# Storing v's rows ahead of a head's loads, and spreading twelve weight pieces over six attention heads

## The chip, the cores and the metric

The kernel runs on one core of a Trainium2 chip. The metric is the time of one execution on the device in microseconds (us). TensorE (PE in the rows) multiplies, VectorE (DVE) and ScalarE (ACT) take the products out of PSUM, GpSimd (POOL) adds in SBUF, and SyncE (SP) issues nearly all DMAs from one queue in program order.

## The reference

One transformer block with conditioning, all in float32, for 2 sequences of 2048 rows of 512 values, 16 heads of 32:

```
ada = silu(c) @ Wada + bada            # shifts, scales and gates
h   = ln(x) * (1 + scale_msa) + shift_msa
q, k, v = h @ Wq + bq, h @ Wk + bk, h @ Wv + bv
A   = softmax(q k^T / sqrt(32))        # per sequence and head
x   = x + gate_msa * (A v @ Wo + bo)
h2  = ln(x) * (1 + scale_mlp) + shift_mlp
out = x + gate_mlp * (gelu(h2 @ W1 + b1) @ W2 + b2)
```

## The kernel before

**Three stages.** The first makes q, k and v in 8 chunks of 512 rows (`chunk`; 12 products `m` each: 4 blocks of q, 4 of k, 4 tiles of v). Every operand is split in a rounded part (`hi`) and a remainder (`lo`), and three matmuls make one product. ACT writes the `hi` part of a q or k block and DVE the `lo` part into one of two slots of `qk_st` (slot m % 2), SP stores both; a v tile goes through one of two slots of `v_st`. So a block waits on ACT until the store of the block two before it has landed (`qk_out`), and a v tile waits on DVE for the store of the tile two before (`v_out`). Beside the last two chunks, `first_max` makes the row maxima of head 0's scores.

**Heads.** The second stage runs 32 heads (`G`; "head" is also the name of a function on each engine), each in 16 steps `t` (128 keys against 2048 queries, four groups `r` of 512 in the four row strips of the array). In a step PE makes four score tiles from four matmuls each (lines 1325, 1327, 1329, 1334), four tiles of the next head's first scores (line 1313, two early in the step and two late), and for the step before the product with v (line 1347); after six of the steps (2, 5, 8, 11, 14, 15) it also makes column sums (line 1338) for that step's tile. ACT takes four exponentials a step (line 835), then the sums if any (line 813). DVE takes four maxima a step (line 1042, "a quad"). GpSimd adds the other ten exponential tiles in place, two instructions a tile (line 686). PE's products of the head stage rotate through 7 PSUM banks by a table (`bank_table`, `USES`) that is computed when the program is written: each use names the bank and the use before it that must be over. `EXTRA_AT` lists steps of head 0 in which a second quad is made, so that the maxima run ahead of the scores.

**Loads of a head.** `load_hi(g)` loads q's and k's rounded part (256 KB and 1 MB), `load_lo(g)` the remainders, `load_v(g)` v. `put_max(g)` sends the maxima to their rows. PE waits for `hi_in` before the first maximum tile of a head and for `lo_in` before its first score. SP works through one list, in which a wait holds back everything behind it.

**Weight pieces.** Wo and W1 (`late`, 12 pieces of 128x512) are needed only in the third stage (projection and MLP). Each is loaded into one of two slots of `tmp3`; ACT rounds it (`split_late_hi`, line 795), then DVE subtracts the rounded part from the piece (`split_late_lo`, line 1074, both inputs in SBUF), and the slot is free. These stand in an engine's program behind the work of a step (`between`): in head 0, steps 2 to 13, one in each. The third stage's first projection waits for all of them.

The third stage is not touched by the change.

Of the kernel before, what the change touches and what calls it, by code (L numbers as in the profile page):

```python
# [31 lines left out]
KC = D // P  # L32
FB = FF // P
CH = 512
TT = CH // P
# [14 lines left out]
HALVES = 2  # L50
FILLS = NQ * NT
LEAD = 3
EXTRA_AT = (2, 6, 10)
BANKS, O_BANK = 7, 7
START = 1

# [8 lines left out]
def bank_table():  # L65

    step, group = 11.7, 3.7  # L70
    until = {"S": (8, 10, 12, 14), "M": (11, 13, 6, 8), "D": 16}
    free = [0] * BANKS
    last = [None] * BANKS
    count = {"S": 0, "M": FILLS, "D": 0}

    def use(kind, at, banks):
        bank = min(banks, key=lambda b: free[b])
        free[bank] = at
        before = last[bank]
        count[kind] += 1  # L80
        last[bank] = (kind, count[kind])
        return bank, before, count[kind]

    now = 0
    heads = []
    for g in range(G):
        steps = []
        for t in range(NT):
            tail = g == G - 1
            banks = range(BANKS)  # L90
            uses = {"extra": [], "max": [None] * NQ, "scores": [None] * NQ, "sums": []}
            if g == 0 and t in EXTRA_AT:
                uses["extra"] = [use("M", now + 6 + 3 * n, banks) for n in range(NQ)]
                now += 8
            for pair, others in ((0, 1), (2, 3)), ((2, 3), (0, 1)):
                for r in pair:
                    uses["scores"][r] = use("S", now + until["S"][r], range(3 + r, 4 + r) if tail else banks)
                if g < G - 2 or g == G - 2 and t < NT - LEAD:
                    for r in others:
                        uses["max"][r] = use("M", now + until["M"][r], banks)  # L100
            tiles = [(t - 1) % NT] if (g or t) and (t - 1) % NT in PE_TILES else []
            groups = [PE_TILES.index(tile) for tile in tiles] + ([ND - 1] if g and t == 1 else [])
            for n, d in enumerate(groups):
                uses["sums"].append((d, *use("D", now + until["D"] + 2 * n, range(2, 3) if tail else banks)))
            now += step + group * len(groups)
            steps.append(uses)
        heads.append(steps)
    end = [(d, *use("D", now, range(2, 3))) for d in (PE_TILES.index(NT - 1), ND - 1)]
    return heads, end
# [6 lines left out]
def block_kernel(nc, x, cT, wq, wk, wv, wo, w1, w2, wada, bqT, bkT, b1T, badaT, bada, bv, bo, b2, out):  # L116
# [7 lines left out]
    with ExitStack() as ctx:  # L124
# [206 lines left out]
        def rows_of(w, c0):  # L331
# [14 lines left out]
        late = [(wo[k * P:(k + 1) * P, :], [wo_r[:, s, k, :] for s in range(2)]) for k in range(KC)]  # L346
        late += [(w1[k * P:(k + 1) * P, at:at + D], [w1_r[:, s, k, at:at + D] for s in range(2)])
                 for k in range(KC) for at in range(0, FF, D)]
        LATE_STEP = 2
        N_CONST = 5  # L350


# [21 lines left out]
        def _(sp):  # L374
# [141 lines left out]
            def store_rec(g):  # L516

                sp.wait_ge(rec_ok, g + 1)
                sp.dma_start(rec_dram[g:g + 1, :].rearrange("o (p x) -> (o p) x", x=NT), rec_c[:]).then_inc(rec_out, 16)

            def head(g):

                sp.wait_ge(b_mm, g * FILLS)
                if g + 2 < G:
                    load_hi(g + 2, (g + 2) % HI_BUF)
                load_sums(g - 1)
                sp.wait_ge(pv_mm, START + g * NT)
                load_lo(g + 1, (g + 1) % TWO)
                load_v(g + 1, (g + 1) % TWO)
                store_rec(g - 1)  # L530
                put_max(g + 1, (g + 1) % TWO)
                store_head(g - 1, (g - 1) % TWO)


            store_qk(NCHUNK - 2, *ORDER[NCHUNK - 2], range(2))
# [6 lines left out]
            store_v(NCHUNK - 2, *ORDER[NCHUNK - 2])  # L542
            sp.wait_ge(qkv_mm, (NCHUNK - 1) * MM_CHUNK)
            load_k(k_hi[0], qk_hi, 0, hi_in[0])
            load_k(k_lo[0], qk_lo, 0, lo_in[0])
            store_qk(NCHUNK - 1, *ORDER[NCHUNK - 1])
            store_v(NCHUNK - 1, *ORDER[NCHUNK - 1], range(1))
            sp.wait_ge(a_max, FILLS)
            load_q(q_hi[0], qk_hi, 0, hi_in[0])
            put_max(0, 0)  # L550
            load_hi(1, 1)
            store_v(NCHUNK - 1, *ORDER[NCHUNK - 1], range(1, TT))
            for k, (rows, _) in enumerate(late):
                if k == 0:
                    sp.wait_ge(ada_mm, ADA)
                if k >= 2:
                    sp.wait_ge(late_hi, k - 1)
                    sp.wait_ge(late_lo, k - 1)
                sp.dma_start(tmp3[:, k % 2, :], rows).then_inc(late_in[k % 2], 16)
                if k == 1:  # L560
                    sp.wait_ge(qkv_mm, NCHUNK * MM_CHUNK)
                    stored(NCHUNK)
                    load_v(1, 1)
                    load_hi(2, 2)
                    load_lo(1, 1)
            put_max(1, 1)
            for g in range(1, G - 2):
                head(g)

# [152 lines left out]
        def _(act):  # L722
# [116 lines left out]
                    if t in between:  # L839
                        between[t]()  # L840

            probs(0, {LATE_STEP + k: lambda k=k: split_late_hi(k) for k in range(len(late))})
            for i in range(2):
                act.wait_ge(v_out[i], START + 16 * NCHUNK * TT // 2)
            for g in range(1, G - 1):
                probs(g)

            def split_first_oT(half):

# [46 lines left out]
        def _(dve):  # L896
# [177 lines left out]
                nc.vector.tensor_tensor(lo, tmp3[:, k % 2, :], hi.bitcast(F32), ALU.subtract).then_inc(late_lo, 1)  # L1074


            head(0, {LATE_STEP + k: lambda k=k: split_late_lo(k) for k in range(len(late))})
            for g in range(1, G - 1):
                head(g)

            def normalise_first(half):
                dve.wait_ge(oT_in, 16 * half + 16)
# [433 lines left out]
```

## Time and profile before

| | |
|---|---|
| median of 3 runs | 2544.93 us (2541.89 to 2549.74) |
| the profiled execution, its own time | 2552.45 us |
| its span in the trace | 2550.7 us |
| PE busy | 2414.3 us (95%) |
| DVE, POOL, ACT busy | 68%, 59%, 56% |

Read it as one engine, PE, that works nearly all the time, and look for the stretches where it doesn't. In the page's 40 slices (64 us each) PE is at 9 tenths but for the first slice, slices 5 to 8 from the left (from about 255 us to 510 us) and the end of the head stage near 2050 us. The granted clock (PEclk) is below full in the same places.

### The profile page before, as it was taken

To read this page: it belongs to the slowest core of one execution; us is meant where nothing else is said; L and a number is where in the kernel's file an instruction comes from. 1 tells how busy PE (TensorE), PEld (TensorE's weight loads), DVE (VectorE), ACT (ScalarE), POOL (GpSimd) and SP (SyncE) were. 2 spreads that over 40 slices of the span, in tenths; PEclk is the share of its full clock that TensorE was granted. 3 is DMA by queue.
4 is the path that set the end of the run, shared out by engine and by line. 5 is a ranking of instruction groups with operands and counts; after the bars stand their busy time and mean duration, and the time that the engine had idled before them with its cause. 6 is when DMAs were issued, how large, how long until landed. Compare 5 with 4: busy or idle time off the path is not lost.

```text
span 2550.7 us, 49502 instructions
## 1 busy us (share of the span) xinstructions
PE 2414.3 (95%) x19544; PEld 1358.2 (53%) x19544; DVE 1745.4 (68%) x2878; ACT 1423.4 (56%) x2622; POOL 1502.3 (59%) x706
## 2 busy tenths in 40 slices
PE   6999855899999999999999999999999888999998
PEld 4788642344444444444444444444444346888887
DVE  4444544788888888887888888788878326666563
ACT  3233203577777777777777777777777542222221
POOL 0000103488788878887887888788878634232330
PEclk9999986799999999999999999999999888999999
DMA  7655532122222222222222222222222111332200
GB/s 268 208 171 186 137 110 89 45 75 58 67 72 71 58 68 72 66 62 69 75 57 66 75 69 57 67 77 62 61 71 74 49 50 39 93 103 68 66 34 34
DMA packets 204948, 210.33 MB, mean 82 GB/s; under 512 B 112384, under 2 KB 145152, under 8 KB 195328
## 3 DMA queue, kind: packets, MB, share of 16 engines
q1 hardware_dynamic: 202224, 205.56, 26.9%
q8 instruction: 143, 2.34, 0.4%
q10 hardware_dynamic: 2512, 1.86, 0.3%
q14 instruction: 69, 0.57, 0.1%
HBM read 146.30 MB, written 60.82 MB: 81 GB/s over the span
## 4 chain that ended last, share of the span: by engine, by line
PE 83%; DMA 8%; DVE 3%; ACT 3%; issue 2%; SPq 1%; POOL 0%; ACTq 0%; POOLq 0%; DVEq 0%
PE ps L1216 19%; PE ps L1347 19%; PE ps L1313 9%; PE ps L1325 9%; PE ps L1456 7%; PE ps L1338 7%; PE ps L1327 5%; PE ps L1329 4%; DMA partial_sums<-work 4%; PE ps L1334 2%; DMA q_lo<-work 2%; DVE part_max L1042 1%; ACT work L813 1%; PE ps L1225 1%; DMA tmp<-in_wo 1%
## 5 line engine op out<-in xcount | busy, mean ns | idle before, releaser
L686 POOL TENSOR_TENSOR work<-work 128x1024 f32<-128x1024 f32 x576 | 1351.5, 2405 | 413.9 <-PE ps L1338 223.1
L1042 DVE TENSOR_REDUCE part_max<-ps 128x1 f32<-128x512 f32 x1984 | 1233.2, 682 | 287.7 <-PE ps L1313 287.5
L835 ACT ACTIVATE work<-ps 128x512 f32<-128x512 f32 x2048 | 1058.4, 603 | 355.2 <-PE ps L1334 323.3
L1347 PE MATMUL ps<-work 128*32 128x512 f32 x4096 | 557.7, 617 | 0.2 <-ACT work L835 0.2
L1313 PE MATMUL ps<-acts_r 32*128 32x512 f32 x1344 | 419.2, 480 | 24.7 <-DVE part_max L1042 18.7
L1216 PE MATMUL ps<-acts_r,weights_r 128*128 128x512 f32 x1536 | 383.6, 400 | 4.9 <-DVE acts_r L962 3.8
L1216 PEld LDWEIGHTS ps<-acts_r,weights_r 128*128 128x128 f32 x1536 | 293.5, 193 | 70.2 <-issue 6.8
L1325 PE MATMUL ps<-acts_r 32*128 32x512 f32 x1408 | 300.9, 475 | 28.9 <-DVE work L975 20.0
L1325 PEld LDWEIGHTS ps<-acts_r 32*128 32x128 f32 x1408 | 145.8, 187 | 339.4 <-DVE part_max L1042 176.6
L1327 PE MATMUL ps<-acts_r 32*128 32x512 f32 x1408 | 260.9, 401 | 0.0
L1313 PEld LDWEIGHTS ps<-acts_r 32*128 32x128 f32 x1344 | 181.5, 186 | 140.5 <-DVE part_max L1042 111.4
L1338 PE MATMUL ps<-work,ones 128*32 128x512 f32 x1792 | 236.8, 600 | 0.0
L1334 PE MATMUL ps<-acts_r,minus_r 1*128 1x512 f32 x1024 | 232.7, 450 | 0.0
L1334 PE MATMUL ps<-m_odd,minus_r 1*128 1x512 f32 x1024 | 227.8, 441 | 0.0
L884 ACT ACTIVATE work<-ps,b_sb 128x512 f32<-128x512 f32 x64 | 44.0, 689 | 309.0 <-PE ps L1216 309.0
L1313 PE MATMUL ps<-acts_r,w_r 32*128 32x512 f32 x640 | 199.0, 474 | 7.0 <-DVE part_max L1042 4.1
L1216 PE MATMUL ps<-weights_r,acts_r 128*128 128x512 f32 x768 | 188.7, 400 | 12.9 <-DVE acts_r L1092 9.9
L659 POOL TENSOR_TENSOR var_eps<-var_eps,mv 128x4 f32<-128x4 f32 x16 | 3.2, 201 | 320.4 <-DVE mv L940 320.4
L1329 PE MATMUL ps<-w_r,acts_r 32*128 32x512 f32 x1024 | 188.2, 402 | 0.0
L1329 PE MATMUL ps<-acts_r 32*128 32x512 f32 x1024 | 186.0, 396 | 0.0
L701 POOL TENSOR_TENSOR work<-work,gate_b 128x512 f32<-128x512 f32 x60 | 85.6, 1456 | 170.0 <-DMA work<-in_x 149.6
L1456 PE MATMUL ps<-w_r,acts_r 128*128 128x512 f32 x768 | 184.4, 391 | 0.0
(88 smaller groups left out, 2542.9 us busy)
## 6 DMA issues: line engine op xcount, KB each, us to landing
acts_r<-k_hi SPq DMA_DIRECT2D x32, 1024.0 KB
acts_r<-k_lo SPq DMA_DIRECT2D x32, 1024.0 KB
work<-in_x SPq DMA_DIRECT2D x16, 1024.0 KB, 5.4
q_hi<-work SPq DMA_DIRECT2D x32, 256.0 KB, 2.6
q_lo<-work SPq DMA_DIRECT2D x32, 256.0 KB, 3.3
k_hi<-work SPq DMA_DIRECT2D x32, 256.0 KB, 2.6
k_lo<-work SPq DMA_DIRECT2D x32, 256.0 KB, 3.2
v_rows<-work SPq DMA_DIRECT2D x32, 256.0 KB, 2.0
```

The lines of the kernel that those rows point to most:

```text
L686: nc.gpsimd.tensor_tensor(psum_acc[:, at], first, prob[:, t % RING, at], ALU.add).then_inc(add_ok, 1)
L835: nc.scalar.activation(prob[:, t % RING, j * CH:(j + 1) * CH], ps[:, bank, :], ACT.Exp, scale=SCALE).then_inc(exp_ok, 1)
L1042: nc.vector.tensor_reduce(part_max[:, r * TT + q // NQ, q % NQ:q % NQ + 1], ps[:, bank, :], AX.X, ALU.max).then_inc(a_max, 1)
L1216: mm = nc.tensor.matmul(o, lhs(s, kk), rhs(r, kk), start=(kk == 0 and s == r), stop=(kk == KC - 1 and s == 1))
L1313: nc.tensor.matmul(ps[:, use[0], :], q_hi[u][at, q // NQ * P:(q // NQ + 1) * P], k_hi[u][at, q % NQ * CH:(q % NQ + 1) * CH], start=True, s ...
L1325: nc.tensor.matmul(o, k_hi[u][at, keys], q_hi[u][at, :], start=True, stop=False)
L1327: nc.tensor.matmul(o, k_lo[w][at, keys], q_hi[u][at, :], start=False, stop=False)
L1329: nc.tensor.matmul(o, k_hi[u][at, keys], q_lo[w][at, :], start=False, stop=False)
L1334: nc.tensor.matmul(o, minus_r[row, :], m_row[w][row, :], start=False, stop=True).then_inc(b_mm, 1)
L1338: mm = nc.tensor.matmul(ps[j * DH:(j + 1) * DH, bank, :], ones[:, 0:DH], src(j), start=True, stop=True)
L1347: mm = nc.tensor.matmul(ps[j * DH:(j + 1) * DH, O_BANK, :], v_sb[g % TWO][:, t, :], prob[:, t % RING, j * CH:(j + 1) * CH], start=(t == 0) ...
L1456: mm = nc.tensor.matmul(ps[:, 4 + t, :], g_r[:, f % 4, s, t * P:(t + 1) * P], w2_r[:, r, f, :], start=(f == 0 and s == r), stop=(f == FB - ...
```

## The change

It does five things. The v stores of the last chunk are issued around `put_max(0)` and ahead of `load_hi(1)`. The last chunk's q stores are issued between `load_k(k_hi[0])` and `load_k(k_lo[0])`. Head 1's v and remainders are loaded ahead of head 2's rounded parts. The twelve weight pieces go two to a head, heads 0 to 5, behind steps 4 and 11 (`LATE_STEPS`), loaded at the end of the SP work of the head before. And head 0 makes no maximum tiles in step 0, and a second quad in steps 3, 6, 9 and 12 in place of 2, 6 and 10.

```diff
-EXTRA_AT = (2, 6, 10)
+EXTRA_AT = (3, 6, 9, 12)
...
-                if g < G - 2 or g == G - 2 and t < NT - LEAD:
+                if (g or t) and g < G - 2 or g == G - 2 and t < NT - LEAD:
...
-        LATE_STEP = 2
+        LATE_STEPS = (4, 11)
+        LATE_HEADS = len(late) // len(LATE_STEPS)
...
+            def load_late(g):
+
+                for k in range(g * len(LATE_STEPS), (g + 1) * len(LATE_STEPS)):
+                    if k >= 2:
+                        sp.wait_ge(late_hi, k - 1)
+                        sp.wait_ge(late_lo, k - 1)
+                    sp.dma_start(tmp3[:, k % 2, :], late[k][0]).then_inc(late_in[k % 2], 16)
+
             def head(g):
...
                 store_head(g - 1, (g - 1) % TWO)
+                if g + 1 < LATE_HEADS:
+                    load_late(g + 1)
...
             load_k(k_hi[0], qk_hi, 0, hi_in[0])
+            store_qk(NCHUNK - 1, *ORDER[NCHUNK - 1], range(KC))
             load_k(k_lo[0], qk_lo, 0, lo_in[0])
-            store_qk(NCHUNK - 1, *ORDER[NCHUNK - 1])
+            store_qk(NCHUNK - 1, *ORDER[NCHUNK - 1], range(KC, 2 * KC))
             store_v(NCHUNK - 1, *ORDER[NCHUNK - 1], range(1))
             sp.wait_ge(a_max, FILLS)
             load_q(q_hi[0], qk_hi, 0, hi_in[0])
+            store_v(NCHUNK - 1, *ORDER[NCHUNK - 1], range(1, 3))
             put_max(0, 0)
+            store_v(NCHUNK - 1, *ORDER[NCHUNK - 1], range(3, TT))
             load_hi(1, 1)
-            store_v(NCHUNK - 1, *ORDER[NCHUNK - 1], range(1, TT))
-            for k, (rows, _) in enumerate(late):
...
-                if k == 1:
-                    sp.wait_ge(qkv_mm, NCHUNK * MM_CHUNK)
-                    stored(NCHUNK)
-                    load_v(1, 1)
-                    load_hi(2, 2)
-                    load_lo(1, 1)
+            sp.wait_ge(ada_mm, ADA)
+            load_late(0)
+            sp.wait_ge(qkv_mm, NCHUNK * MM_CHUNK)
+            load_v(1, 1)
+            load_lo(1, 1)
+            load_hi(2, 2)
+            stored(NCHUNK)
             put_max(1, 1)
+            load_late(1)
...
-            probs(0, {LATE_STEP + k: lambda k=k: split_late_hi(k) for k in range(len(late))})
+            def late_pieces(g):
+                first = g * len(LATE_STEPS)
+                return {t: lambda k=first + i: split_late_hi(k) for i, t in enumerate(LATE_STEPS) if g < LATE_HEADS}
+
+            probs(0, late_pieces(0))
...
-            head(0, {LATE_STEP + k: lambda k=k: split_late_lo(k) for k in range(len(late))})
-            for g in range(1, G - 1):
-                head(g)
+            for g in range(G - 1):
+                first = g * len(LATE_STEPS)
+                head(g, {t: lambda k=first + i: split_late_lo(k) for i, t in enumerate(LATE_STEPS) if g < LATE_HEADS})
```

On SP, at the end of the last chunk, the list stood like this before; `v_rows` is where v is stored, `q_hi` and `k_hi` are where a head's parts are loaded from, `max_T` the maxima, and `in_wo` a weight piece:

```order
L430 DMA v_rows<-work 128x512
L482 DMA acts_r<-q_hi 128x1x512
L500 DMA acts_r<-max_T 4x4x32 x4
L482 DMA acts_r<-q_hi 128x1x512
L478 DMA acts_r<-k_hi 128x1x2048
L430 DMA v_rows<-work 128x512 x3
L559 DMA tmp<-in_wo 128x512 x2
```

and now:

```order
L431 DMA v_rows<-work 128x512
L483 DMA acts_r<-q_hi 128x1x512
L431 DMA v_rows<-work 128x512 x2
L501 DMA acts_r<-max_T 4x4x32 x4
L431 DMA v_rows<-work 128x512
L483 DMA acts_r<-q_hi 128x1x512
L479 DMA acts_r<-k_hi 128x1x2048
L528 DMA tmp<-in_wo 128x512 x2
```

The last three v tiles are stored ahead of head 1's q and k, the weight pieces still behind them.

On DVE, from the end of head 0 to the middle of head 1, the list stood like this before (`part_max` is a maximum, x4 a quad, `weights_r` the subtraction of a weight piece, `sums_c` and `den_c` the denominators of step 8):

```order
L994 STREAM_TRANSPOSE max_T<-row_max 128x32
L1074 TENSOR_TENSOR weights_r<-tmp,weights_r 128x512
L1042 TENSOR_REDUCE part_max<-ps 128x1 x4
L1074 TENSOR_TENSOR weights_r<-tmp,weights_r 128x512
L1042 TENSOR_REDUCE part_max<-ps 128x1 x44
L1052 TENSOR_REDUCE den_c<-sums_c 128x16
```

and now:

```order
L1006 STREAM_TRANSPOSE max_T<-row_max 128x32
L1054 TENSOR_REDUCE part_max<-ps 128x1 x32
L1086 TENSOR_TENSOR weights_r<-tmp,weights_r 128x512
L1054 TENSOR_REDUCE part_max<-ps 128x1 x16
L1064 TENSOR_REDUCE den_c<-sums_c 128x16
L1066 RECIPROCAL rec_c<-den_c 128x16
L1054 TENSOR_REDUCE part_max<-ps 128x1 x12
L1086 TENSOR_TENSOR weights_r<-tmp,weights_r 128x512
```

The two last subtractions of head 0 are gone, and head 1 has one between the quads of steps 4 and 5 and one between those of steps 11 and 12. Heads 2 to 5 read as head 1.

## Rows read from the trace of the kernel before

**Rows 1.** The page: busy time by engine, share of the span, instructions.

```profile
PE 2414.3 (95%) x19544; PEld 1358.2 (53%) x19544; DVE 1745.4 (68%) x2878; ACT 1423.4 (56%) x2622; POOL 1502.3 (59%) x706
```

**Rows 2.** Busy time by stretches: from, to, length, engines, PEclk, DMA share, GB/s.

```profile
330.00:340.00 10.00, 0.00 (x0) 0.00 (x0) 0.00 (x0) 0.67 (x1) 0.00 (x0) 0.50 0.23 93
...
560.00:680.00 120.00, 119.25 (x1212) 53.66 (x1208) 97.64 (x165) 90.33 (x173) 103.88 (x45) 1.00 0.25 70
```

**Rows 3.** Timeline, last chunk: start, length, engine, line, [idle before <-releaser].

```profile
310.53 0.58 SPq L478 DMA_DIRECT2D acts_r<-k_hi  x1
...
339.33 0.69 ACT L763 ACTIVATE work<-ps,bq_sb 128x512 fp32r<-128x512 f32 x1 [22.00 <-DMA q_lo<-work]
...
341.45 0.79 PE L1256 MATMUL ps<-acts_r 96*128 96x512 f32 x1 [18.31 <-DVE part_max L980]
...
345.74 0.43 SPq L425 DMA_DIRECT2D q_lo<-work  x1
...
356.56 0.69 ACT L763 ACTIVATE work<-ps,bq_sb 128x512 fp32r<-128x512 f32 x1 [3.05 <-PE ps L1216]
```

**Rows 4.** Timeline, from the last chunk to head 0.

```profile
374.52 0.55 SPq L478 DMA_DIRECT2D acts_r<-k_hi  x1
375.11 18.55 SPq L430 DMA_DIRECT2D v_rows<-work  x3
392.61 0.69 DVE L975 TENSOR_TENSOR work<-ps,work 128x512 f32<-128x512 f32 x1 [21.07 <-DMA v_rows<-work]
393.40 0.79 PE L1325 MATMUL ps<-acts_r 32*128 32x512 f32 x2 [19.99 <-DVE work L975]
```

**Rows 5.** Timeline, first step of heads 1 and 4: the output of the head before.

```profile
497.07 0.60 ACT L801 ACTIVATE work<-ps 128x512 f32<-128x512 f32 x1 [0.19 <-PE ps L1338]
...
648.38 0.60 ACT L801 ACTIVATE work<-ps 128x512 f32<-128x512 f32 x1 [0.28 <-PE ps L1338]
```

**Rows 6.** Timeline, head 0: the wait for a late piece, and pieces beside GpSimd.

```profile
429.57 0.63 ACT L795 ACTIVATE weights_r<-tmp 128x512 fp32r<-128x512 f32 x1 [10.30 <-DMA tmp<-in_wo]
...
453.58 0.69 DVE L1074 TENSOR_TENSOR weights_r<-tmp,weights_r 128x512 fp32r<-128x512 f32 x1 [0.46 <-ACT weights_r L795]
...
475.41 7.44 POOL L686 TENSOR_TENSOR work<-work 128x1024 f32<-128x1024 f32 x3 [4.05 <-ACT work L835]
...
478.23 2.42 DVE L1074 TENSOR_TENSOR weights_r<-tmp,weights_r 128x512 fp32r<-128x512 f32 x1 [2.01 <-ACT weights_r L795]
...
481.30 0.79 PE L1313 MATMUL ps<-acts_r,w_r 32*128 32x512 f32 x1 [3.59 <-DVE part_max L1042]
...
487.61 1.94 PE L1347 MATMUL ps<-work 128*32 128x512 f32 x8
...
491.50 1.06 PE L1347 MATMUL ps<-work 128*32 128x512 f32 x8
```

**Rows 7.** Timeline, head 3, steps 3 to 5, and its GpSimd work.

```profile
607.30 37.45 POOL L686 TENSOR_TENSOR work<-work 128x1024 f32<-128x1024 f32 x16 [1.15 <-ACT work L835]
...
608.92 2.48 DVE L1042 TENSOR_REDUCE part_max<-ps 128x1 f32<-128x512 f32 x4 [1.10 <-PE ps L1313]
...
609.75 2.07 ACT L835 ACTIVATE work<-ps 128x512 f32<-128x512 f32 x4 [0.64 <-POOL work L686]
...
610.11 1.06 PE L1347 MATMUL ps<-work 128*32 128x512 f32 x8
...
611.66 2.48 DVE L1042 TENSOR_REDUCE part_max<-ps 128x1 f32<-128x512 f32 x4 [0.25 <-PE ps L1313]
...
612.83 1.06 PE L1347 MATMUL ps<-work 128*32 128x512 f32 x8
```

**Rows 8.** Timeline, head 2, around the denominators of step 8.

```profile
571.29 1.06 PE L1347 MATMUL ps<-work 128*32 128x512 f32 x8
...
572.51 0.35 DVE L1052 TENSOR_REDUCE den_c<-sums_c 128x16 f32<-128x112 f32 x1
...
574.18 1.07 PE L1347 MATMUL ps<-work 128*32 128x512 f32 x8
```

More of the change, by code:

```diff
@@ L549, in _ @@
             load_q(q_hi[0], qk_hi, 0, hi_in[0])
+            store_v(NCHUNK - 1, *ORDER[NCHUNK - 1], range(1, 3))
             put_max(0, 0)
+            store_v(NCHUNK - 1, *ORDER[NCHUNK - 1], range(3, TT))
             load_hi(1, 1)
-            store_v(NCHUNK - 1, *ORDER[NCHUNK - 1], range(1, TT))
-            for k, (rows, _) in enumerate(late):
[L554 to L559, printed above, removed]
-                if k == 1:
-                    sp.wait_ge(qkv_mm, NCHUNK * MM_CHUNK)
-                    stored(NCHUNK)
-                    load_v(1, 1)
-                    load_hi(2, 2)
-                    load_lo(1, 1)
+            sp.wait_ge(ada_mm, ADA)
[5 more added lines that the diff above has]
+            stored(NCHUNK)
             put_max(1, 1)
+            load_late(1)
             for g in range(1, G - 2):
@@ L845, in _ @@
             for g in range(1, G - 1):
-                probs(g)
+                probs(g, late_pieces(g))
             def split_first_oT(half):
```

## The prediction

> **What bounds the kernel now.** I read the page first: PE is busy 2414.3 us, 95% of the span [rows 1], so only stretches in which PE waits or runs slowly can give time. The stretches show which those are: from 560 us on, in the middle of the heads, PE works 119.25 of 120 us at full clock, with POOL busy 103.88 and DVE 97.64 [rows 2]. That part has nothing to give, and anything added to it that reaches PE is a loss. Then I read the timeline where PE is idle.
>
> Three waits stand out, all behind 1 MB loads. First, in the last chunk, ACT waits 22.00 us for a store of q and PE 18.31 us [rows 3]: SP issued head 0's k_hi and k_lo at 310.5 us, and the q stores land behind both. Second, PE waits 19.99 us for the last v tile, because the v stores, issued from 375.1 us, stand behind head 1's q_hi and k_hi (374.5); the v tile is taken at 392.6 [rows 4]. Third, in head 0 ACT waits 10.30 us for a weight piece behind two more such loads [rows 6]. After each wait the granted clock is at its lower level, 0.50, which is 1.2 GHz [rows 2].
>
> A head in the steady part takes (648.38 - 497.07) / 3 = 50.4 us, while head 0 takes 497.07 - 393.40 = 103.7 us, both up to the same instruction in the next head [rows 4, 5]. So head 0 holds 53 us of loss, and 12 weight pieces.
>
> My unit for loads: from the issue of k_hi(1) at 374.52 to the v tile at 392.61 are 18.1 us for 1.25 MB, or 14 us for 1 MB with its start [rows 4].
>
> **Term 1, q stores between k_hi(0) and k_lo(0): -6 us.** The first q store now waits for 1 MB and not 2. ACT resumed at 339.3; it will at about 326, 13.3 us earlier. The k_lo load is then issued behind the fourth q store, at 345.7 - 13.3 = 332.4, later by the issue, about 333, and lands with the store behind it at about 348.6. The block that needs that store is the seventh; ACT took it at 356.56 [rows 3], 343.3 when moved by 13.3. So it comes 5.3 us late, and PE waits about 4.7 for it (in the wait that we have, 22.00 us less the usual 3.05 make ACT 18.95 us late and PE waits 18.31, 0.6 less). The second wait costs a second stretch at the lower clock, some 5 us with half the speed, 2.5 us. 13.3 - 4.7 - 2.5 = 6. Range 3 to 10.
>
> **Term 2, v stores first: -4 us.** This step does what it says and gains little. The second v store is now issued at about 369.5 and only q_hi(0), 256 KB, is ahead of it; the last v tile is taken at about 374.5, and head 0 begins there, not at 393.4. But step 1 needs head 1's q_hi and k_hi, whose issue moves from 374.5 to about 376. They were the load that all had to wait for, and they still take 14 to 17 us: step 1 begins at about 393. What is saved is one step 0, 4 us at the lower clock. The wait for the v store becomes a wait for `hi_in`.
>
> **Term 3, head 0 without ten pieces and the 10.30 us wait: -29 us.** From step 1 at 393 to the output in head 1: a steady head is 50.4 us, less step 0 and plus the part of the next head's step 0 up to its output, nearly equal. Four extra quads of 2.48 us against 1.10 us of DVE idle in a step with sums [rows 7]: 5.5. Two pieces at 5.0 (below): 10. Lower clock at the start and behind the extra quads: 4.7, my choice between nothing and the 10 us or so of four stretches like the one priced below. Sum 70.6, so it ends at 463.6, against 497.07: 33.5 earlier, 4 of them term 2. Head 2's loads, 2.5 MB behind head 1's, land at about 431, before step 13 needs them at about 447. Range of terms 2 and 3: 26 to 41.
>
> **Term 4, ten pieces in heads 1 to 5: +50 us.** This decides. In step 4 of a steady head [rows 7], ACT ends its exponentials at 609.75 + 2.07 = 611.8. The rounding, 0.63 us, ends at 612.45, and DVE, free since 608.92 + 2.48 = 611.4, has waited. Its next quad was due at 611.66. The subtraction then meets GpSimd. Row 478.23 shows what happens: GpSimd ran three additions of 2.34 us from 475.41, with ends at 477.75 and 480.1; the subtraction started at 478.23 and took 2.42 us, to 480.65, 0.55 behind the end of an addition, where one with GpSimd idle took 0.69 [rows 6]. The eleven others of head 0 read the same way. In a steady head GpSimd adds without a gap from 607.30 for 37.45 us, sixteen additions, over steps 4 and 11 both [rows 7]. The one that runs at 612.5 ends at 614.3; the subtraction ends at 614.9, and the quad is 3.2 us late.
>
> What PE has in hand against that is almost nothing. The denominators put 0.6 us on DVE, which has 0.25 us idle a step, and PE's step grew from 612.83 - 610.11 = 2.72 to 574.18 - 571.29 = 2.89 [rows 7, 8]. The reason is in the bank table: in step 5 the last maximum tile takes the bank of the first one of the same step. So PE waits about 3.1 us. By row 481.30, where the subtraction was held too, it was 3.59 us. Then the clock: behind that wait a step took 491.50 - 487.61 = 3.89 us, mostly at the lower level, against 2.72 [rows 6], and such a stretch lasts one or two steps, 1.2 to 2.5 us. Sum 5.0 a piece. At step 11 GpSimd is on its queue of additions as well, with a delay by the same count of about 3.0 us. Ten pieces: 50 us. Bounds: no meeting with GpSimd leaves the quad 1.5 us late, 15 us for ten; a full addition of delay each time and two slow steps is 57.
>
> The Trainium skill (SBUF — State Buffer, "SBUF: two separate sides") has the rule: GpSimd and a VectorE instruction with two SBUF inputs share a pair of ports, whichever starts first holds it for its whole instruction, and the other is blocked. The trace agrees, 2.42 against 0.69 us. By the rule each moved piece is exposed, since GpSimd is busy 103.88 of 120 us in a steady stretch [rows 2]; without it the ten would cost about 15 us and the change would be a gain of 24.
>
> **Parts at nothing.** ACT's 0.63 us of rounding lies in its idle 0.6 us before the next exponentials (without it, +0.6 us a piece, hidden behind DVE's delay). The loads of pieces, 512 KB a head, are issued near step 12, when the head's own 2.5 MB (34 us by my unit) are in; were they late, ACT would wait as at 429.57. SP's new waits in `load_late` are for steps 4 and 11, over by `put_max` at step 12, so nothing queues behind them. The bank table repeats as before from head 3 on.
>
> **Sum.** -6 - 4 - 29 + 50 = +11 us on the profiled execution's 2552.45. The median of the runs shown is 7.5 us below that execution; I carry the difference over: 2544.9 + 11 = 2556.
>
> **The rivals.** *A, forecast: pieces cost about 5 us each in the steady heads, and outweigh head 0's gain.* Chance 0.5; -5 to +20 us.
> *B, the clock holds.* If the waits of 3.1 us don't bring the lower clock, or only for a moment, term 4 is 31 and the sum -8: 2537. For it: the steady heads run at 1.00 throughout [rows 2], so the engine is well used before each wait. Against it: the wait of 3.59 us in head 0 was followed by matmuls at half speed, 1.94 us for the eight of line 1347 that take 1.06 otherwise [rows 6]. Chance 0.15.
> *C, the pieces hide, and the change is faster.* The place is the subtraction behind step 4: if the phase of GpSimd's additions is such that one ends as DVE asks, the quad is 1.5 to 2 us late and term 4 is about 20 to 25. The sum is then -16: 2529. It decides below a price of 3.9 us a piece (39 us gained over ten). For it: PE's waits shift PE against GpSimd and may open gaps. Against it: additions have no gap from 607.3, so the phase at step 4 is the same in each head. Chance 0.15.
> *D, head 0 gives less.* If the second wait in the last chunk is as long as the first, or the lower clock holds through head 0's extra quads as it did before, terms 1 to 3 give 25 and the sum is +25: 2570. For it: head 0 has 53 us of loss before, and what of it belongs to its pieces, to its three extra quads and to the clock I can't separate. Chance 0.2.
>
> **How the numbers follow.** The predicted time is A's, 2556. The range, 2529 to 2573, takes in B, most of C and D. About 0.3%, 7.6 us, is what a measurement of this kernel can tell from no change. Faster by more needs -8 or less: most of C and half of B, 0.2. Within: the lower part of A and the rest of B, 0.22. Slower: 0.58.
>
> **What would show it.** Right: PE's wait before the first step of head 0 gone, one of about 15 us before line 1313's first tile of head 1; ACT's wait for a q store near 10 us and a second of about 5; head 0 to its output in about 70 us from step 1; subtractions of 2 to 3 us in heads 1 to 5, each followed by a PE wait near 3 us on a maximum; heads 1 to 5 about 60 us long, later ones 50.4; PEclk below full between 500 and 750 us. Wrong: subtractions of 0.69 us there, or heads 1 to 5 under 57 us long.

## The result

| | median us | lowest to highest | ratio to before, 95% interval |
|---|---|---|---|
| before, 4 runs beside the others | 2543.41 | 2540.25 to 2549.74 | |
| the changed kernel, 4 runs | 2572.94 | 2566.53 to 2576.44 | 1.0109 [1.0083, 1.0135] |

The change makes the kernel about 28 us slower by the ratio (the two medians are 29.5 us apart). The two profiled executions are nearer to each other: 2569.98 us after (span 2568.2) against 2552.45 before, +17.5. The one of before lies about 9 us above the median of this table, the one of after 3 below; what follows divides up the 17.5.

From the page of the changed kernel, busy time by engine, which answers to [rows 1]:

```profile
PE 2416.8 (94%) x19544; PEld 1356.7 (53%) x19544; DVE 1760.0 (69%) x2878; ACT 1424.0 (55%) x2622; POOL 1506.1 (59%) x706
```

PE does the same work and has 15 us more idle time in a longer span. DVE is 15 us busier with the same 2878 instructions: some of them take longer. To find where, I took the marker of [rows 5], the output of a head in the first step of the next, after head 0 and after head 5 (timeline of the changed kernel):

```profile
470.48 0.60 ACT L809 ACTIVATE work<-ps 128x512 f32<-128x512 f32 x1 [0.21 <-PE ps L1350]
...
771.61 0.60 ACT L809 ACTIVATE work<-ps 128x512 f32<-128x512 f32 x1 [0.26 <-PE ps L1350]
```

The first stands at 497.07 us before [rows 5]: 26.6 us are gained up to there. Heads 1 to 5 then take 62.4, 58.2, 62.0, 60.2 and 58.2 us, 301.1 together, against 250.9 before: +50.2. Heads 6 to 31 come out 4.7 us shorter, 2.4 of it in the last one (single heads vary from 49.7 to 51.0 us in either trace, the last two apart), what is behind them 1.4. The sum is -26.6 + 50.2 - 4.7 - 1.4 = +17.5.

The timeline of the last chunk, which answers to [rows 3]:

```profile
309.88 0.59 SPq L479 DMA_DIRECT2D acts_r<-k_hi  x1
...
328.88 0.69 ACT L771 ACTIVATE work<-ps,bq_sb 128x512 fp32r<-128x512 f32 x1 [12.19 <-DMA q_lo<-work]
...
331.00 0.80 PE L1268 MATMUL ps<-acts_r 96*128 96x512 f32 x1 [8.50 <-DVE part_max L992]
...
335.77 0.56 SPq L479 DMA_DIRECT2D acts_r<-k_lo  x1
...
356.29 0.69 ACT L771 ACTIVATE work<-ps,bq_sb 128x512 fp32r<-128x512 f32 x1 [13.59 <-DMA k_lo<-work]
...
358.42 0.79 PE L1268 MATMUL ps<-acts_r 96*128 96x512 f32 x1 [9.95 <-DVE part_max L992]
```

One wait of PE became two, 8.50 and 9.95 us, 18.45 together against 18.31. ACT takes its seventh block at 356.29, where it took it at 356.56.

From there to head 0, which answers to [rows 4]:

```profile
376.76 0.69 DVE L987 TENSOR_TENSOR work<-ps,work 128x512 f32<-128x512 f32 x1 [3.57 <-DMA v_rows<-work]
377.56 0.81 PE L1337 MATMUL ps<-acts_r 32*128 32x512 f32 x4 [2.49 <-DVE work L987]
378.49 0.54 SPq L479 DMA_DIRECT2D acts_r<-k_hi  x1
...
398.52 0.80 PE L1337 MATMUL ps<-acts_r 32*128 32x512 f32 x2 [18.88 <-DMA acts_r<-k_hi]
```

Head 0 begins at 377.56 and not at 393.40, does step 0, and waits 18.88 us for head 1's k_hi. Step 1 begins at 398.52. Before it began at 397.49, 4.1 us behind 393.40.

The twelve subtractions together (group of the line: shortest, median, longest in ns, first and last start in us), and the first of head 1 with what follows it:

```profile
L1086 DVE TENSOR_TENSOR weights_r<-tmp,weights_r x12: 1117/2448/4897, 416.4 to 752.5; 128x512 fp32r<-128x512 f32 x12
```

```profile
481.57 7.45 POOL L694 TENSOR_TENSOR work<-work 128x1024 f32<-128x1024 f32 x3
...
484.27 2.53 DVE L1086 TENSOR_TENSOR weights_r<-tmp,weights_r 128x512 fp32r<-128x512 f32 x1 [0.95 <-ACT weights_r L803]
...
487.46 0.79 PE L1325 MATMUL ps<-acts_r,w_r 32*128 32x512 f32 x1 [3.02 <-DVE part_max L1054]
...
488.18 1.94 PE L1359 MATMUL ps<-work 128*32 128x512 f32 x8
```

This is the forecast's chain, link by link: DVE waits for ACT's rounding, the subtraction is held beside GpSimd's additions, PE waits 3.02 us for the maximum behind it, and the next matmuls run at the lower level, 1.94 us against 1.06. The piece of step 11 in the same head shows something that the forecast did not have:

```profile
505.05 9.34 POOL L694 TENSOR_TENSOR work<-work 128x1024 f32<-128x1024 f32 x4
...
510.50 4.44 DVE L1086 TENSOR_TENSOR weights_r<-tmp,weights_r 128x512 fp32r<-128x512 f32 x1 [0.89 <-ACT weights_r L803]
...
515.60 0.79 PE L1325 MATMUL ps<-acts_r,w_r 32*128 32x512 f32 x1 [4.88 <-DVE part_max L1054]
...
516.46 1.08 ACT L843 ACTIVATE work<-ps 128x512 f32<-128x512 f32 x2 [4.78 <-PE ps L1346]
...
517.62 2.35 POOL L694 TENSOR_TENSOR work<-work 128x1024 f32<-128x1024 f32 x1 [3.22 <-ACT work L843]
```

GpSimd's four additions end at 507.4, 509.7, 512.1 and 514.4 us (9.34 / 4 each). The subtraction was there from 510.50, yet it did not end 0.55 us behind the addition that was running (512.1) but 0.55 behind the next (514.4): 514.94. Two of the ten pieces in heads 1 to 5 went so, with 4.44 and 4.90 us; the others took 1.7 to 2.5. Both times the subtraction ended only when GpSimd had no addition left: here its next one came at 517.62, after 3.22 us without work, because ACT's exponentials had waited 4.78 us for PE, and PE for the quad behind the subtraction.

Over heads 1 to 5 as a stretch (columns as in [rows 2]), and the ten microseconds around the wait of 4.88 us:

```profile
480.00:740.00 260.00, 228.77 (x2151) 99.45 (x2151) 197.81 (x298) 165.85 (x316) 185.84 (x79) 0.91 0.23 67
```

```profile
510.00:520.00 10.00, 5.12 (x36) 1.28 (x28) 7.27 (x7) 2.64 (x5) 6.75 (x3) 0.68 0.00 0
```

PE works 88% of it and not 99%, and its granted clock is 0.91 on average where the steady part had 1.00.

### The profile page after: what moved, and what is told of

The parts are those of the page before. It is cut to its first block, busy times and chain, and to the rows that moved or that the text cites. A ratio compares the mean times of both kernels' runs of the same rounds, so it can differ in the third digit from the quotient of the medians.

```text
span 2568.2 us, 49501 instructions
## 1 busy us (share of the span) xinstructions
PE 2416.8 (94%) x19544; PEld 1356.7 (53%) x19544; DVE 1760.0 (69%) x2878; ACT 1424.0 (55%) x2622; POOL 1506.1 (59%) x706
## 4 chain that ended last, share of the span: by engine, by line
PE 81%; DMA 7%; DVE 4%; ACT 3%; issue 2%; POOL 1%; SPq 1%; ACTq 0%; POOLq 0%; DVEq 0%
PE ps L1359 18%; PE ps L1228 18%; PE ps L1325 9%; PE ps L1337 9%; PE ps L1350 7%; PE ps L1468 7%; PE ps L1339 5%; PE ps L1341 4%; DMA partial_sums<-work 3%; PE ps L1346 2%; DVE part_max L1054 1%; DMA q_lo<-work 1%; ACT work L843 1%; DVE weights_r L1086 1%; ACT work L821 1%
## 5 line engine op out<-in xcount | busy, mean ns | idle before, releaser
L843 ACT ACTIVATE work<-ps 128x512 f32<-128x512 f32 x2048 | 1059.0, 602 | 395.2 <-PE ps L1346 364.5
L1228 PE MATMUL ps<-weights_r,acts_r 128*128 128x512 f32 x768 | 187.6, 398 | 14.8 <-DVE acts_r L1104 11.8
L821 ACT ACTIVATE work<-ps 128x512 f32<-128x512 f32 x224 | 134.3, 599 | 92.5 <-PE ps L1350 83.9
```

What stands on the lines that cost most here:

```text
L843: nc.scalar.activation(prob[:, t % RING, j * CH:(j + 1) * CH], ps[:, bank, :], ACT.Exp, scale=SCALE).then_inc(exp_ok, 1)
L1228: mm = nc.tensor.matmul(o, lhs(s, kk), rhs(r, kk), start=(kk == 0 and s == r), stop=(kk == KC - 1 and s == 1))
```

## The experiments

### Which half of the change costs, and what a piece's price is made of

**e1: the pieces alone.** The order of SP, the quads and head 0's step 0 of before, the pieces spread as in the change.

```diff
-EXTRA_AT = (3, 6, 9, 12)
+EXTRA_AT = (2, 6, 10)
...
             load_k(k_hi[0], qk_hi, 0, hi_in[0])
-            store_qk(NCHUNK - 1, *ORDER[NCHUNK - 1], range(KC))
             load_k(k_lo[0], qk_lo, 0, lo_in[0])
-            store_qk(NCHUNK - 1, *ORDER[NCHUNK - 1], range(KC, 2 * KC))
+            store_qk(NCHUNK - 1, *ORDER[NCHUNK - 1])
...
             load_hi(1, 1)
+            store_v(NCHUNK - 1, *ORDER[NCHUNK - 1], range(1, TT))
...
```

> The kernel before with only the weight pieces moved: two to a head behind steps 4 and 11 of heads 0 to 5; stores, loads and extra quads as before. Theory (the moved pieces are the loss): heads 1 to 5 take about 60 us each from output to output, 50 us more together, and head 0 gets back 20 to 30 us, so the time is about 2543 + 25 = 2568 us. Rival (the new order of stores and loads, not the pieces, loses): 2543 us or less, heads 1 to 5 near 50 us.

Measured: 2570.77 us, 1.0097 [1.0067, 1.0127]. Its first output is at 464.4 us, 32.7 before that of [rows 5], and heads 1 to 5 take 299.4 us, +48.5. So the pieces alone make the loss, and they also bring all of head 0's gain, 6 us more of it than the whole change.

**e2: the order alone.** The change, with the twelve pieces back in head 0's steps 2 to 13.

```diff
-        LATE_STEPS = (4, 11)
-        LATE_HEADS = len(late) // len(LATE_STEPS)
+        LATE_STEPS = tuple(range(2, 14))
+        LATE_HEADS = 1
...
             load_hi(2, 2)
             stored(NCHUNK)
+            load_late(range(2, len(late)))
...
```

> The changed kernel with all twelve pieces back in head 0, steps 2 to 13; stores, loads and extra quads as changed. Theory (pieces are the loss, the new order gains a little): heads 1 to 5 at 50 us, head 0 longer than in the changed kernel by about 30 us, time about 2540 to 2550 us. Rival (the order loses): over 2560 us.

Measured: 2552.02 us, 1.0021 [1.0008, 1.0034]. The first output is at 499.8 us, 2.8 later than before, and the heads behind it take 50.0. In its last chunk ACT waits 12.2 and 14.2 us, and PE waits 20.3 us for head 1's k_hi. The new order gains nothing; with the pieces in head 0 it is a loss of 0.1 to 0.3%.

**e3: the same place, one SBUF input.** DVE reads only the piece, in a maximum along its rows, in place of the subtraction. The remainders of Wo and W1 are left out.

```diff
-                nc.vector.tensor_tensor(lo, tmp3[:, k % 2, :], hi.bitcast(F32), ALU.subtract).then_inc(late_lo, 1)
+                nc.vector.tensor_reduce(scrap[:, k:k + 1], tmp3[:, k % 2, :], AX.X, ALU.max).then_inc(late_lo, 1)
```

> The changed kernel with the subtraction of a weight piece on VectorE replaced by a maximum over the same 512 elements of the loaded piece: the same place, the same wait for ScalarE, but one input in SBUF in place of two; the remainders of Wo and W1 are left out. Theory (the port pair shared with GpSimd is the larger part): the instruction takes 0.6 to 0.7 us each time, the quad behind it is 1.5 us late, heads 1 to 5 take 53 to 55 us each, time about 2572 - 28 = 2545 us. Rival (the wait for ScalarE in VectorE's program is the cost, the port is not): instruction short, heads still near 60 us, time within 5 us of the changed kernel.

Measured: 2536.51 us, 0.9959 [0.9940, 0.9978]. The group of its line, and the stretch of heads 1 to 5:

```profile
L1087 DVE TENSOR_REDUCE scrap<-tmp x12: 685/686/689, 416.8 to 720.0; 128x1 f32<-128x512 f32 x12
```

```profile
480.00:740.00 260.00, 246.96 (x2444) 108.73 (x2446) 203.57 (x341) 189.14 (x360) 203.86 (x87) 0.98 0.25 70
```

Twelve instructions of 685 to 689 ns beside the same additions of GpSimd: with one SBUF input none is held. Heads 1 to 5 take 268.5 us, 32.7 less than with the subtraction, 3.3 us a piece.

**e4: the subtraction on GpSimd.** It stands there ahead of the additions of two of the steps; DVE has no piece in its program.

```diff
+            def split_late_lo(k):
+                pool.wait_ge(late_hi, k + 1)
+                hi, lo = late[k][1]
+                nc.gpsimd.tensor_tensor(lo, tmp3[:, k % 2, :], hi.bitcast(F32), ALU.subtract).then_inc(late_lo, 1)
+
             for g in range(G - 1):
-                sum_probs(g)
+                first = g * len(LATE_STEPS)
+                sum_probs(g, {t: lambda k=first + i: split_late_lo(k) for i, t in enumerate((6, 12)) if g < LATE_HEADS})
```

> The changed kernel with the subtraction of a weight piece done by GpSimd, ahead of its additions of tiles 6 and 12, and nothing of it on VectorE. Theory: VectorE has neither the wait nor the port conflict, GpSimd takes 1.2 us more twice a head and has 8 us idle in one, so heads 1 to 5 take 50 to 52 us and the time is about 2572 - 45 = 2527 us. Rival (ScalarE's 0.6 us or the loads of pieces are part of the cost): heads 1 to 5 over 55 us. Rival (GpSimd becomes the bound): ScalarE waits for GpSimd's additions in steps 8 to 15, heads 1 to 5 at 53 to 55 us.

Measured: 2513.98 us, 0.9868 [0.9839, 0.9898].

```profile
L699 POOL TENSOR_TENSOR weights_r<-tmp,weights_r x12: 1287/1306/1349, 425.6 to 705.3; 128x512 fp32r<-128x512 f32 x12
```

```profile
480.00:740.00 260.00, 259.21 (x2631) 116.36 (x2635) 211.92 (x356) 201.68 (x387) 233.85 (x105) 1.00 0.26 76
```

PE works 259.21 of 260 us at full clock, and heads 1 to 5 take 248.8 us, no more than heads without a piece. This is the zero against which the others are priced: the subtraction on DVE costs 301.1 - 248.8 = 52.3 us, 5.2 a piece, of which 3.3 is the meeting with GpSimd (e3 against the change) and 2.0 is what DVE's slot costs without it (e3 against e4): a wait for ACT's rounding, and 0.69 us of work.

### Is the rest the wait for ACT, and is the order worth anything without the pieces?

**e5: DVE's part a step later.** ACT rounds behind step 4 as before; DVE subtracts behind step 5.

```diff
-                head(g, {t: lambda k=first + i: split_late_lo(k) for i, t in enumerate(LATE_STEPS) if g < LATE_HEADS})
+                head(g, {t + 1: lambda k=first + i: split_late_lo(k) for i, t in enumerate(LATE_STEPS) if g < LATE_HEADS})
```

> The changed kernel with VectorE's subtraction one step later (steps 5 and 12) while ScalarE's rounding stays at 4 and 11: VectorE no longer waits for ScalarE, but still needs the port pair. Theory (two costs add: about 1.8 us a piece for the wait behind ScalarE, about 3.3 us for the port): the first goes, heads 1 to 5 take 50 + 2 x 3.3 = 56 to 57 us, time about 2572 - 17 = 2555 us. Rival (the place makes the port wait, a wait for ScalarE moves the subtraction onto a fresh addition): heads near 53 us, 2540. Rival (nothing gained, since the port wait ends with an addition whenever it starts): heads 59 to 61 us.

Measured: 2562.95 us, 1.0058 [1.0036, 1.0080]; heads 1 to 5 take 294.8 us, 6.3 less than in the change, where the theory wanted some 17. Its subtractions as a group:

```profile
L1086 DVE TENSOR_TENSOR weights_r<-tmp,weights_r x12: 821/1907/7381, 418.6 to 739.0; 128x512 fp32r<-128x512 f32 x12
```

The wait for ACT is gone. But the ten pieces of heads 1 to 5 now fall into two kinds. The five behind step 5 took 0.82 to 0.88 us: each started about 0.3 us before an addition ended. The five behind step 12 took 7.30 to 7.38 us: each started 0.14 to 0.24 us after an addition had begun, and was held over that one and the two behind it, until GpSimd had none left. One of the long ones with what followed it, then one of the short ones, and the stretches around a short and a long one (timeline of e5, and columns as in [rows 2]):

```profile
502.55 7.35 DVE L1086 TENSOR_TENSOR weights_r<-tmp,weights_r 128x512 fp32r<-128x512 f32 x1
...
510.56 0.79 PE L1325 MATMUL ps<-acts_r 32*128 32x512 f32 x1 [6.47 <-DVE part_max L1054]
...
512.58 2.36 POOL L694 TENSOR_TENSOR work<-work 128x1024 f32<-128x1024 f32 x1 [3.23 <-ACT work L843]
...
540.07 0.88 DVE L1086 TENSOR_TENSOR weights_r<-tmp,weights_r 128x512 fp32r<-128x512 f32 x1
```

```profile
530.00:556.00 26.00, 25.63 (x260) 11.37 (x254) 21.79 (x37) 20.14 (x40) 24.83 (x11) 1.00 0.31 86
556.00:582.00 26.00, 19.51 (x176) 8.45 (x172) 21.24 (x26) 12.81 (x26) 15.16 (x7) 0.80 0.13 39
```

PE waits 0.3 us behind a short one and 6.4 to 6.5 us behind a long one. So e5's loss against e4, 46 us or 9.2 a head, lies nearly all behind step 12, and the same subtraction on DVE behind step 5 costs next to nothing. Neither of the two rivals had that: heads of 58.2 to 60.4 us look like the last one, but the price is not the same whenever the instruction starts. One piece a head behind step 5, over twelve heads, was not run.

**e6: the old order, with GpSimd's subtraction.** The edit of e4 on top of e1.

> The kernel before with the pieces spread and subtracted on GpSimd; stores, loads and extra quads as before. With the fourth run it tells what the new order of stores, loads and quads is worth when the pieces cost nothing. Theory (the new order trades its waits one for one, -4 us by the prediction's terms 1 and 2 and +3 to +6 by the comparison of the first two runs): within 6 us of the fourth run's 2514, ACT's wait for a q store again near 22 us and the v wait near 20, no wait on head 1's k_hi. Rival (the new order is worth its 10 us): 2524 us or more.

Measured: 2510.03 us, 0.9866 [0.9844, 0.9888], beside 0.9868 for e4. ACT waits 23.7 us for the q store and DVE 22.2 us for the v store, much as before the change (22.0 and 21.1).

**e7: e4 with both k loads ahead of the q stores.**

```diff
             load_k(k_hi[0], qk_hi, 0, hi_in[0])
-            store_qk(NCHUNK - 1, *ORDER[NCHUNK - 1], range(KC))
             load_k(k_lo[0], qk_lo, 0, lo_in[0])
-            store_qk(NCHUNK - 1, *ORDER[NCHUNK - 1], range(KC, 2 * KC))
+            store_qk(NCHUNK - 1, *ORDER[NCHUNK - 1])
```

> The fourth run's kernel with one thing undone: both k loads of head 0 go ahead of the last chunk's q stores again. Theory (two waits of 12 to 14 us in place of one of 22: term 1 is nothing or a loss): one ACT wait of 22 to 24 us there, time equal to the fourth run's 2514 or up to 5 us less. Rival (term 1 as predicted): 6 us more, 2520.

Measured: 2508.53 us, 0.9850 [0.9827, 0.9872]. With one wait of ACT of 22.1 us in place of two of 12.7 and 14.7 it is, if anything, 5 us faster than e4; the intervals overlap. Term 1 of the forecast, -6, isn't there.

With e1, e2, e4 and e6 the change is taken apart:

| ratio to before | pieces in head 0, on DVE | spread, on DVE | spread, on GpSimd |
|---|---|---|---|
| old order | 1 | 1.0097 (e1) | 0.9866 (e6) |
| new order | 1.0021 (e2) | 1.0109 (the change) | 0.9868 (e4) |

Each step down is 0.0002 to 0.0021; the effect lies in where the pieces stand and which engine subtracts. Pieces in head 0 with the subtraction on GpSimd were not run, so how much of the gain is the spreading and how much the engine is not split up.

### Why the new order gives nothing: the 1 MB loads

In the wait of the last chunk of before, from 325 us, k's two parts are under way, with the q stores behind them (stretch of before; a k load writes 32 rows of k to four groups of 32 partitions, in one transfer):

```profile
325.00:335.00 10.00, 0.00 (x0) 0.00 (x0) 0.00 (x0) 0.00 (x0) 0.00 (x0) 0.59 0.25 102
```

The DMA share is 0.25, four of 16 engines, at 102 GB/s. The changed kernel has the same 0.25, at 83 GB/s, while it waits for head 1's k_hi:

```profile
386.00:396.00 10.00, 0.00 (x0) 0.00 (x0) 0.00 (x0) 0.00 (x0) 0.00 (x0) 0.50 0.25 83
```

The Trainium skill (DMA: Bandwidth & Descriptors, "Why a DMA increments its semaphore by 16 and not by 1") has a rule for it: a transfer runs on the largest number of engines, up to 16, that divides the slowest dimension of both its sides. For this pattern, whose slowest dimension is the four copies, that is four; the trace agrees, 0.25. So I cut the load in four of 32 rows each.

**e8: e4 with every k load in four transfers.** The counts that PE waits for go up with it.

```diff
-LOADS_HI, LOADS_LO, LOADS_0 = 2, 3, 6
+LOADS_HI, LOADS_LO, LOADS_0 = 5, 6, 6
...
-                rows = src[1][g * DH:(g + 1) * DH, :].rearrange("(o d) q -> o d q", o=1).broadcast_to((NQ, DH, L))
-                sp.dma_start(dst.bitcast(F32), rows).then_inc(done, 16)
+                for r in range(NQ):
+                    sp.dma_start(dst[r * DH:(r + 1) * DH, :].bitcast(F32), src[1][g * DH:(g + 1) * DH, :]).then_inc(done, 16)
```

> The fourth run's kernel with each 1 MB k load issued as four transfers of 32 rows in place of one whose outermost dimension is the fourfold repeat. Theory (one transfer of k uses 4 of the 16 DMA engines, and every wait at the start of the heads is 14 to 20 us long for that): a k load lands in 4 to 6 us, the waits for q stores, k stores and head 1's k_hi fall to under 5 us each, and the time is about 2514 - 35 = 2480 us, if SyncE's 0.55 us for each more issue (24 more a head) stays hidden. Rival (the source's bandwidth bounds the load, not the number of engines): waits within 3 us of the fourth run's, same time. Rival (the loads now take all 16 engines and the partial sums' small transfers wait behind them): heads longer than 50 us.

Measured: 2568.96 us (2547.96 to 2583.91, 12 runs), 1.0081 [1.0055, 1.0106]. The first output came at 431.2 us, 37 earlier than in e4, but the heads behind it take 50.1 to 55.0 us, 52.7 on average and not 50.1 (the last two left out), which takes it all back and more. The wait for head 1's k_hi is 12.0 us, not the under 5 that were expected. The chain that ended last says which transfer is in the way (shares of the span by line):

```profile
PE ps L1227 18%; PE ps L1358 18%; DMA partial_sums<-work 10%; PE ps L1336 9%; PE ps L1324 9%; PE ps L1467 7%; PE ps L1349 6%; PE ps L1338 5%; PE ps L1340 4%; PE ps L1345 2%; ACT work L827 1%; DVE part_max L1060 1%; PE ps L1236 1%; DMA q_lo<-work 1%; DMA work<-in_x 0%
```

The small store of a head's column sums stands in the chain once a head, with 7 to 9.5 us each, 10% in all; in e4 it has 4%. My reading is that the wide loads now keep all 16 engines busy, so that this store finds none free; no run changed that store alone.

**e9: only the first loads in four.** k's rounded part for heads 0 to 2 and its remainder for heads 0 and 1; the single transfer from there on.

```diff
-            def load_k(dst, src, g, done):
+            def load_k(dst, src, g, done, split_heads=3):
+                if g < split_heads:
+                    for r in range(NQ):
+                        sp.dma_start(dst[r * DH:(r + 1) * DH, :].bitcast(F32), src[1][g * DH:(g + 1) * DH, :]).then_inc(done, 16)
+                    return
...
```

> The fourth run's kernel (pieces spread, subtracted on GpSimd, the changed order) with the 1 MB k loads of heads 0, 1 and 2 alone issued as four transfers of 32 rows; from head 3 on single transfers. Theory (the eighth run gained 37 us at the start and lost more in the heads, because its small partial sums waited behind loads on all 16 engines): first output at about 431 us, heads at 49.7 to 50 us, time about 2511 - 37 = 2475 us. Rival (the loss in the heads comes from SyncE's issues or from the first heads' loads): heads over 51 us, time over 2490 us.

Measured: 2481.92 us, 0.9754 [0.9738, 0.9770]. First output at 431.7 us, heads 1 to 5 of 49.8 us. In the last chunk ACT's wait for the q store is gone and that for the k store is 4.4 us, where e4 had 12.7 and 14.7; PE's wait for k_hi is 12.2 us, where e4 had 23.3 (timeline of e9):

```profile
355.37 1.90 SPq L481 DMA_DIRECT2D acts_r<-k_hi  x4
...
367.89 0.79 PE L1341 MATMUL ps<-acts_r 32*128 32x512 f32 x2 [12.21 <-DMA acts_r<-k_hi]
```

**e10: q's first loads in four too.**

```diff
+                if g < split_heads:
+                    for r in range(NQ):
+                        sp.dma_start(dst[r * DH:(r + 1) * DH, :].bitcast(F32), src[0][g * DH:(g + 1) * DH, r * CH:(r + 1) * CH]).then_inc(done, 16)
+                    return
...
```

> The same with the 256 KB q loads of those heads in four transfers too. Theory (q's loads also use 4 of 16 engines and stand ahead of k's): PE's wait for head 1's parts falls from 12 us by some 3 us, time 3 us less than the run with k alone, about 2472 us. Rival (the wait is then SyncE's issue time, 0.35 to 0.5 us a transfer): no less, or more.

Measured: 2475.84 us (2475.06 to 2476.90), 0.9722 [0.9709, 0.9735], the fastest of all. The first loads as a stretch, and the wait for k_hi:

```profile
310.00:316.00 6.00, 6.00 (x28) 4.85 (x27) 5.03 (x8) 1.38 (x2) 0.00 (x0) 1.00 1.00 251
```

```profile
361.79 0.79 PE L1345 MATMUL ps<-acts_r 32*128 32x512 f32 x2 [7.31 <-DMA acts_r<-k_hi]
```

All 16 engines, 251 GB/s, and a wait of 7.31 us where e4 had 23.27 and the change 18.88.

**e11: e9 in the old order.** The edits of e1 and e9 on e4.

> The kernel before with the pieces spread and subtracted on GpSimd and the same split loads of heads 0 to 2, in the old order of stores, loads and quads. It tells what the new order is worth once a load is short. Theory (the order trades waits one for one while each load is 15 to 20 us; with loads of 5 us the old order still has both k loads ahead of the q stores and head 1's parts ahead of the v stores): 5 to 10 us more than the new order, about 2482 us. Rival (the order is worth nothing in either case): within 4 us of the new order's.

Measured: 2486.28 us, 0.9765 [0.9749, 0.9781]. DVE waits 14.8 us for the v store. The new order is 4.4 us faster (e9) in this setting, which the overlapping intervals don't quite settle.

## Why the prediction was right, and where it was not

The direction was right, and so was the mechanism of the loss. The time is in the range by luck: 2572.94 against 2556 (2529 to 2573) is 0.06 us inside the upper end, and two of the four executions lie above it. It was rival D, with a chance of 0.2, that came true, and not forecast A: D had terms 1 to 3 give 25 us and not 39, through a second wait in the last chunk as long as the first; the trace shows that wait, and 26.6 us up to head 0's output. D's +25 stands against +23.6 up to the end of head 5.

**Term 4, ten pieces, +50: right.** Measured +50.2 between the two traces, and 52.3 with e4 as the zero. The chain was as described, and the wait per piece on average too: 3.2 us, forecast 3.1. What I had not foreseen is its spread: five waits of 3.0 us behind step 4 (forecast 3.1), but behind step 11 three of 2.4 and two of 4.88 and 5.29, where the piece was held over two additions. That the five average 3.5, near the 3.0 that I had put there, is luck. The lower bound was too low: "no meeting with GpSimd leaves the quad 1.5 us late, 15 us for ten". Without the meeting e3 still lost 19.7 us, since a late quad of 1.5 us costs clock too (0.98). Rivals B and C fall for the change: the clock did not hold (0.91), and no PE wait was under 2.4 us. But C's mechanism exists: e5's five pieces behind step 5 each met the end of an addition and hid. The argument against C, that the phase is the same in each head, holds in e5 as well; there it is the good phase that repeats.

**Term 3, head 0 without ten pieces, -29: right.** Forecast from step 1 to the output 70.6 us; measured 470.48 - 398.52 = 72.0. That is 31.7 less than the 103.7 of before, of which 4.1 are step 0: 27.6.

**Term 2, v stores first, -4: right in mechanism, nothing gained.** The wait for the v store did become one for `hi_in`. But the unit of 14 to 17 us was too small: k_hi(1) was issued at 378.49 and PE went on at 398.52, 20.0 us later (23.6 in e4). The load no longer had the queue nearly for itself: two weight pieces and v, 768 KB, were issued right behind it, at 379.08 to 380.08 us, and the first ten us of the wait read

```profile
380.00:390.00 10.00, 0.00 (x0) 0.00 (x0) 0.00 (x0) 3.05 (x5) 0.00 (x0) 0.50 0.64 128
```

with more than k_hi's quarter of the engines at work. That they slow k_hi down fits, but no run held them back.

**Term 1, q stores between the two k loads, -6: wrong.** The step that failed is "it comes 5.3 us late, and PE waits about 4.7 for it". ACT resumed at 328.88 (forecast 326) and then waited 13.59 us, PE 9.95. Behind the step is "my unit for loads": 14 us for 1 MB, taken from one wait. Both k loads run on four engines at 83 to 102 GB/s, by my estimate from these rates 10 to 13 us each for the bytes alone; from the issue of one alone to the block that needs a store behind it passed 19.0 us (309.88 to 328.88) and 20.5 (335.77 to 356.29), against 28.8 for both in a row before [rows 3]. So two parted loads take 10.7 us more than the two in a row; that this is a start paid twice is my reading. Terms 1 and 2, forecast at -10, came to +1.0: step 1 at 398.52 where it was 397.49.

The forecast's sum of terms was +11 and the traces say +17.5. The 6.5 between them are 11.0 in terms 1 and 2 and 1.6 in terms 3 and 4, less the 4.7 and 1.4 behind head 5. The median is off by more, 2572.94 - 2556 = 16.9, because I had carried over 7.5 us between the profiled execution and the median of before: behind the change the profiled execution lay 3.0 us below its median, not above.

**Open.** What decides that DVE's instruction is held over one addition or over two or three is not shown. In all eight cases (two in the change, one in e1, five in e5) it was held until GpSimd had no addition left; in the others it was held over one at most, and where another was queued that one then took 2.8 us and not 2.36. Why 1 MB on four engines came at 83 GB/s in one place and 102 in another I did not separate, nor how much of the 18 to 24 us is start or other loads. That the store of sums in e8 is late because no DMA engine is free was argued, not tried.

## What to carry to other kernels

Work that is taken off a starved start has to go to an engine and a place that have time for it in the steady part: here DVE's 0.69 us cost PE 5.2 us each, while the same subtraction, as 1.3 us on GpSimd, cost nothing and turned +1% into -1.3%. And price it place by place, not by the average: a step later, the same DVE instruction cost nearly nothing in one half of the head and 9 us in the other. Look at the DMA share of a stretch in which everything waits for one load: here 0.25 said that the transfer's shape, not its place in the queue, was what to change. And make a load wide only where something waits for it: done in all heads, the heads grew from 50.1 to 52.7 us and the gain was gone.

## What the runs showed of the hardware

- A DVE instruction with two SBUF inputs was held by GpSimd's additions: in the change most often until 0.55 us behind the end of the one that ran, but in two of ten until behind the next (4.44 and 4.90 us), and in five of ten in e5 until behind the third (7.30 to 7.38 us). Each of these longer ones, and one in e1 (4.91), ended 0.55 us behind the last addition before GpSimd ran out of them. An addition that follows such a subtraction directly took 2.8 us in place of 2.36. The Trainium skill (SBUF — State Buffer, "SBUF: two separate sides") gives the port to whichever starts first; the trace agrees that it is held for a whole instruction, but it also shows that one who waits can be passed over by later ones. With one SBUF input nothing was held, 0.685 to 0.689 us in all twelve.
- Waits of PE of 2.4 to 5.3 us, one about every 25 us, brought the mean granted clock from 1.00 to 0.91 over 260 us; matmuls behind such a wait ran at 1.2 GHz (1.94 us for what takes 1.06). Waits of 1.1 to 1.3 us in the same places left it at 0.98 (e3), waits of 0.3 us at 1.00 (e5, 530 to 556 us).
- The load of 1 MB as a copy to four groups of partitions used a quarter of the DMA engines (share 0.25, 83 to 102 GB/s); as four transfers all of them (1.00, 251 GB/s).
